# Turning masked logits and attention weights: ordinary fp32 products with the identity in place of the transposing form

## What is computed

```python
h = (x @ W).reshape(N, H, C)
alpha_s = einsum('nhc,hc->nh', h, a_src);  alpha_d = einsum('nhc,hc->nh', h, a_dst)
e = leaky_relu(alpha_s[src] + alpha_d[dst], 0.2)
m = segment_max(e, dst)
ex = exp(e - m[dst]);  den = segment_sum(ex, dst)
out = segment_sum(h[src] * (ex / den[dst])[:, :, None], dst)
```

## Time and profile before

| | |
|---|---|
| median of 3 plain runs | 8691.24 us |
| span of the profiled execution | 10523.1 us |
| gathers of the message pass | 1617 instructions |
| gathers of three attention passes | 4851 instructions |
| HBM read, written | 367.38 MB, 25.63 MB |
| POOL busy in the span | 6521.8 us (62%) |
| TensorE busy in the span | 5795.2 us (55%) |

### The profile page before, as it was taken

The page is one execution under the profiler, slowest core; times in us unless marked ns, Lnnn a source line. Parts: engine busy times, 40 slices in busy tenths (PEclk is TensorE's granted clock), DMA queues, the critical chain, the costliest instruction groups (busy, mean ns, idle before and its releaser), DMA issues. The chain is left out here.

```text
span 10523.1 us, 129592 instructions
## 1 busy us (share of the span) xinstructions
PE 5795.2 (55%) x27752; PEld 5101.0 (48%) x27752; DVE 4507.0 (43%) x11640; ACT 3562.3 (34%) x7369; POOL 6521.8 (62%) x6545
## 2 busy tenths in 40 slices
PE   4666666676755555545545555555554545545453
PEld 2155555665644444444444544444444444444443
DVE  6644545455533333333343333333334333333335
ACT  3611111111233333333333333333333333333333
POOL 3455666666366666666656666666665666666665
PEclk6555555555556666666666666666666666666666
DMA  4211111111111111111121111111112111111111
GB/s 130 49 32 36 39 38 39 38 39 39 29 35 34 35 34 34 34 35 34 34 34 35 34 34 34 34 34 35 34 32 36 34 35 34 34 35 34 34 34 30
DMA packets 290251, 394.16 MB, mean 37 GB/s; under 512 B 176393, under 2 KB 183961, under 8 KB 287985
## 3 DMA queue, kind: packets, MB, share of 16 engines
q0 software_dynamic: 206976, 330.75, 16.5%
q1 hardware_dynamic: 61176, 46.25, 1.8%
q10 hardware_dynamic: 22024, 16.47, 0.7%
HBM read 367.38 MB, written 25.63 MB: 37 GB/s over the span
## 5 line engine op out<-in xcount | busy, mean ns | idle before, releaser
L637 POOL DMA_INDIRECT store<-table_a,idx x4851 | 4835.4, 997 | 2626.8 <-issue 1595.4
L1262 PE MATMUL ps<-ident,work 128*128 128x128 f32 x4872 | 1179.2, 417 | 2359.3 <-issue 2226.4
L1279 PE MATMUL ps<-store,work 128*128 x9744 | 1788.8, 355 | 1176.6 <-ACT work L1211 841.1
L1279 PEld LDWEIGHTS ps<-store,work 128*128 128x128 f32 x9744 | 1655.2, 263 | 1379.5 <-issue 1377.7
L778 POOL DMA_INDIRECT store<-table_m,idx x1617 | 1597.5, 988 | 1130.6 <-issue 554.9
L1262 PEld LDWEIGHTS ps<-ident,work 128*128 128x128 f32 x4872 | 928.6, 218 | 2456.7 <-issue 2336.8
L1218 ACT ACTIVATE work<-work,small 128x896 f32<-128x896 f32 x696 | 724.5, 1041 | 3314.6 <-issue 2135.0
L1155 DVE SCALAR_TENSOR_TENSOR work<-dstf,store,select 128x224 f32 x696 | 314.2, 451 | 3116.2 <-issue 1668.3
L1144 DVE CUSTOM_DVE_ANT_0 work<-work,ps 128x896 f32<-128x896 f32 x696 | 756.8, 1087 | 1258.7 <-issue 937.7
L1270 PE MATMUL ps<-ident,work 128*128 128x128 f32 x4872 | 1100.6, 398 | 105.7 <-issue 73.9
L870 PE MATMUL ps<-work 128*128 128x96 f32 x3248 | 817.6, 443 | 615.0 <-DVE work L1058 439.8
(11 more groups left out here) (250 smaller groups left out, 4865.7 us busy)
## 6 DMA issues: line engine op xcount, KB each, us to landing
store<-table_a,idx POOLq DMA_INDIRECT x4851
store<-table_m,idx POOLq DMA_INDIRECT x1617
work<-edge_parts ACTq DMA_DIRECT2D x232, 45.5 KB
edge_parts<-store SPq DMA_DIRECT2D x6, 1617.0 KB, 11.7
work<-edge_parts SPq DMA_DIRECT2D x50, 192.0 KB
table_a<-work SPq DMA_DIRECT2D x12, 606.0 KB, 6.5
work<-table_b ACTq DMA_DIRECT2D x232, 12.0 KB
idx<-in_src_dram SPq DMA_DIRECT2D x116, 28.0 KB
```

The lines of the kernel that those rows point to most:

```text
L637: pool.indirect_dma_start(rows[:, k % RING, j, 0:width], None, table, bass.IndirectOffsetOnAxis(ap=idx[:, k // CHUNK, at:at + 1], axis=0)) ...
L1262: last = pe.transpose(ps[:, 4 + j // 4, (j % 4) * P:(j % 4 + 1) * P], prob[:, par, j, :], ident[:])
L1279: last = pe.matmul(ps[:, 6 + par, 0:D + 1], probT[:, par, j, :], rows_of(at("slot", 3))[:, j, 0:D + 1], start=(j == 0), stop=(j == TPG - 1))
```

## The change

In `turn_probs` and `turn_mask` the call `pe.transpose` becomes `pe.matmul` with the same operands: the tile is the stationary operand, the identity (fp32, 128 by 128) the moving one. The product is the same transposed tile. Waits, semaphores, banks and order stay as they are. The turns of other blocks (L1379, L1571 and those of the list's making) are left in the transposing form.

```diff
@@ turn_probs
                     for j in range(TPG):
-                        last = pe.transpose(ps[:, 4 + j // 4, (j % 4) * P:(j % 4 + 1) * P], prob[:, par, j, :], ident[:])
+                        last = pe.matmul(ps[:, 4 + j // 4, (j % 4) * P:(j % 4 + 1) * P], prob[:, par, j, :], ident[:], start=True, stop=True)
                     last.then_inc(s["pt_ready"], 1)
@@ turn_mask
                     for j in range(TPG):
-                        last = pe.transpose(ps[:, 2 * par + j // 4, (j % 4) * P:(j % 4 + 1) * P],
-                                            masked[:, par, j].rearrange("p h n -> p (h n)"), ident[:])
+                        last = pe.matmul(ps[:, 2 * par + j // 4, (j % 4) * P:(j % 4 + 1) * P],
+                                         masked[:, par, j].rearrange("p h n -> p (h n)"), ident[:], start=True, stop=True)
                     last.then_inc(s["t_ready"], 1)
```

## The result

The changed kernel takes 9186.3 us (median of 4 runs, 9175.16 to 9194.86) against 8691.01 us before: a ratio of 1.058 with a 95% interval of 1.0563 to 1.0596. It is slower by 495 us.

The account below looks back on a forecast made before the run. The prediction took POOL's gathering as the bound nearly all the time. Turns adding 1.5 + 0.8 = 2.3 us, less 1.4 us slack, left 0.9 us, 0.45 a group; times 696 is 313 us: 8691 + 313 = 9004, said as 9010, range 8650 to 9400.

Parts of the forecast that it names:

- the path from landing to turned masks: In attention, from a group's gathered data landing to its masks being turned; claimed to grow by 2.3 us.
- the slack of POOL's pacing: In attention, masks are turned before POOL ends its next group; claimed to absorb 1.4 us of added path.
- 8.65 us a group: Pace of plain runs over 892 message and attention groups, just under POOL's back-to-back 8.75 us.
- POOL's standing: POOL's 3.4 us stand per two groups, claimed to be mostly a thing of the profiled execution.
- 977 us outside the steady stretches: Start, first 32 groups, between passes and end in the profile; subtracted from the plain 8691 us, leaving 7714.
- 14 products at the low clock: Turn of weights in ordinary form at 1.2 GHz: 3.2 us, 1.5 us more than seven transposing products.
- The turn of masks: Same sizes as the turn of weights, right behind unbroken products that raise the clock; claimed 0.8 us more.
- a loop of two groups: The loop closing over `t_ready`; each group pays half of the remaining 0.9 us, 0.45 us.
- the gathers hide it: Rival: path growth in attention stays within about the slack, so the time is 8691 us, within 20; 24%.
- TensorE becomes the bound: Rival: the clock stays low, an attention step asks 9.7 us of TensorE, giving 9420 us; 17%.
- the clock pays: Rival: 2.4 GHz in most of the attention step shortens weighted sums, a group gains 0.35 us: 8450 us; 14%.
- The span of 11,320 us: Profiled execution of the changed kernel: no slack left, 348 pairs each grow by about 2.3 us, 800 us in all.

Follow-up runs that it names:

- second profile: The kernel before the change, unchanged, run and profiled once more: 8696.0 us, with a profiled span of 8694.1 us.
- both_lead2: The changed kernel with POOL allowed to gather one group further ahead of the turned masks (lead 2 in place of 1): 8699.87 us, ratio 1.0007.
- transposes_twice: The kernel before, with every transposing product of the two turns made twice in the same place, none in the ordinary form: 9105.92 us, ratio 1.0505.
- filler_all: The changed kernel plus 50 unneeded transposing products a pair, spread over each of TensorE's idle stretches: 8708.72 us, ratio 1.0029.
- ordinary_second: The kernel before with ordinary products only in TensorE's second step of each pair, transposing form in the first: 9203.17 us, ratio 1.0615.
- filler_split: The changed kernel plus unneeded transposing products, 10 at each pair's end and 22 behind the next pair's work-list reading: 9102.26 us, ratio 1.0479.

## Why the prediction was right, and where it was off

**The direction and the mechanism.** I forecast 9010 us, 8650 to 9400, slower at 62%; measured 9186 us. The mechanism was the forecast one for about 385 of the 495 us: the turns lengthen the path from landing to turned masks, beyond the slack of POOL's pacing. The other 102 us, gathers that last longer, the forecast had at nothing: it did not name them.

**The reading of the plain kernel held.** I worked out 8.65 us a group and took POOL's standing as a thing of that one profiled execution. The second profile shows 8.79 us and no standing. It was the step I trusted least, and all depended on it. That the number came so near has luck in it. I took 977 us outside the steady stretches from the slow execution, where the second profile has 733; and I gave all 892 groups one pace, where a group of the message pass takes 9.38 us (1866 / 199) and one of attention 8.79. With 733 the one pace would be 8.92, too long; with 977 it came out too short. The two errors offset in part.

**The turns.** 14 products at the low clock: forecast 3.2 us, measured 3.35. The turn of masks: forecast +0.8 us, measured 2.39 against 1.70 in the median of the first steps, +0.7. The growth of the path was forecast as 2.3 us; measured 9.60 - 7.30 = 2.30 us. It comes in one step of two only: the other grows by 0.2 us, since its turns run at the high clock. I had let every step grow and shared the cost over a loop of two groups, which gives the same number; the sharing is not what the trace shows.

**The term that failed is the slack.** I put it at 1.4 us, from the end of the turn to the end of POOL's next group; the rows give 1.46 (6127.47 - 6126.01). POOL does not start at once: with the masks turned at 6015.24 it gathers from 6016.03, 0.79 us later, which is also the median of the pass, where a gather behind another needs only 0.30. So some 0.5 us of the slack was never there. A pair pays 2.3 - 1.46 + 0.49 = 1.33 us, and 348 pairs 463 us; with my 0.9 us a pair it was 313. Measured is 2 x 0.71 = 1.42 us a pair, but only 385 / 348 = 1.11 us of it is standing; 102 / 348 = 0.29 us is gathers that last longer, a term that the sum does not have. The corrected sum comes near the total partly because it is too high for the one and has nothing for the other.

**Rivals.** That the gathers hide it failed by the first step alone; in the second step, at 7.30 us, they did hide it. That TensorE becomes the bound is refuted by both_lead2. (My reading of the earlier trace rows there was loose: one of the 13 products at 6060.5 is the tail of the weighted sums and twelve are turns, and only these have 128 columns, not the whole six microseconds before the rise.) That the clock pays was half right: it rose from 0.67 to 0.83 and shortened the weighted sums by 555 us of busy time, none of it on the path. The span of 11,320 us that I gave for a profiled execution was wrong, as it started from an execution that was not like the others; the changed kernel's was 9193.0 us.

**The two rules.** The Trainium skill's advice in Perfetto Trace Analysis (Optimizing Tensor Performance, Transposes) to make a transpose as a transpose was borne out: two instructions for a tile in place of one. But transposes_twice shows that the form itself is the small part (0.75% of the time); the number of instructions at the low clock is the large one (5.05%). The fear that ordinary products might be needed for the clock fell: transposing ones hold it at 1.00 in filler_all.

## What to carry to other kernels

An engine with a third of its time idle can still set the pace, if a semaphore that it counts up releases the bound engine: measure the path to that semaphore, and add the time that the released engine needs to start again (0.79 us here). For the same reason a higher average clock says little; ask at which clock the burst on the path starts. If a pacing wait has room in its buffers, one more group of lead makes the kernel indifferent to such changes (9186 us to 8700 us here), at no cost measured.

## What I had not expected

- The low clock is not tied to a place. Shortening or filling one step moved the slow burst to the other (ordinary_second, filler_split), at 535 and 420 us of loss.
- 50 unneeded products a pair, some 17,400 in the kernel, made the changed kernel 5% faster, since the clock went from 0.83 to 1.00.
- Half of the edit, in one step of each pair, costs 438 or 535 us, about as much as all of it; half of it the other way, one turn of two in every step, 135 or 200 us.
- A fifth of the loss is no wait at all: the gathers of the same number and size are busy 102 us longer, and the long ones overlap VectorE's L1165.
